# A two-layer graph network: the leaky step and the float16 split of z moved from the middle stage into layer 1

## The reference, cut to what matters

```
x = layernorm(x + L0(x, adj))                       # x: 8 x 2048 x 64
# layer 1: 8 batches x 4 heads = 32 instances of attention over 2048 nodes
h    = einsum('bnc,hdc->bhnd', x, Wh)
s    = where(mask, h h^T, -1e16)
cat  = softmax(s) h + bh                            # per instance 2048 x 64
z    = leaky_relu(cat, 0.2)                         # = max(cat, 0.2 cat)
# middle stage
h2   = einsum('bnk,dk->bnd', z, Wo)                 # 256 -> 64 columns
# layer 2: 8 instances of the same attention, one per batch
out2 = softmax(where(mask, h2 h2^T, -1e16)) h2 + bo
out  = layernorm(leaky_relu(out2, 0.2)) * gamma + beta
x    = layernorm(x + out)
```

## Time and profile before

| | us |
|---|---|
| three runs, median (lowest to highest) | 3323.97 (3322.51 to 3327.71) |
| the profiled execution, its time | 3323.41 |
| its span, first to last instruction | 3321.7 |
| PE busy | 3065.0 (92% of the span) |
| DVE busy | 2739.8 (82%) |
| ACT busy | 2369.3 (71%) |
| POOL busy | 2546.0 (77%) |
| granted clock of PE, mean | 0.976 of full speed |

### The profile page before, as it was taken

One profiled execution on the slowest core, in us unless ns is written; L12 is line 12 of the kernel. 1 busy time (PEld: TensorE's weight loads), 2 busy tenths in 40 slices (PEclk: granted clock), 3 DMA queues, 4 the chain that ended last, 5 costly groups with the idle time before them and its releaser, 6 DMA issues. The chain is left out here.

```text
span 3321.7 us, 126248 instructions
## 1 busy us (share of the span) xinstructions
PE 3065.0 (92%) x49399; PEld 2287.0 (69%) x49399; DVE 2739.8 (82%) x5344; ACT 2369.3 (71%) x2806; POOL 2546.0 (77%) x1861
## 2 busy tenths in 40 slices
PE   5856799999999999999999999999986699999997
PEld 3425577777777777777777777777765577777775
DVE  6664688888888888888888888888877599898998
ACT  1146677777777777777777777777766588787886
POOL 1136598989999999899999999999976257676775
PEclk8979999999999999999999999999998899999998
DMA  5207889998899889999988998899867433332321
GB/s 207 67 1 271 223 156 153 165 161 163 155 164 169 157 156 173 159 159 161 167 164 155 163 166 165 154 166 166 163 122 235 165 124 134 119 130 115 132 116 73
DMA packets 1189166, 507.67 MB, mean 153 GB/s; under 512 B 1090718, under 2 KB 1148508, under 8 KB 1186588
## 3 DMA queue, kind: packets, MB, share of 16 engines
q1 hardware_dynamic: 1187564, 497.60, 70.8%
q0 software_dynamic: 1200, 3.93, 0.3%
HBM read 102.12 MB, written 62.91 MB: 50 GB/s over the span
## 5 line engine op out<-in xcount | busy, mean ns | idle before, releaser
L633 POOL TENSOR_TENSOR mask_slot<-probs 128x1024 f16<-128x1024 f32 x1024 | 1916.1, 1893 | 221.8 <-ACT probs L1017 138.4
L1017 ACT ACTIVATE probs<-scores,shifted_max 128x2048 f32<-128x2048 f32 x512 | 1026.1, 2004 | 166.6 <-DVE shifted_max L1222 159.0
L1217 DVE CUSTOM_DVE_ANT_0 scores<-ps,mask 128x1024 f32<-128x1024 f32 x512 | 625.5, 1222 | 202.4 <-PE ps L860 196.5
L859 PE MATMUL ps<-operands 128*128 128x512 f16 x2048 | 777.3, 380 | 1.7 <-DVE neg_max L1217 1.7
L860 PE MATMUL ps<-operands 128*128 128x512 f16 x2048 | 776.7, 379 | 0.0
L1022 ACT COPY probsT<-ps 128x1024 bf16<-128x1024 bf16 x512 | 518.0, 1012 | 359.3 <-PE ps L868 359.3
L1217 DVE CUSTOM_DVE_ANT_0 scores<-ps,mask,neg_max 128x1024 f32<-128x1024 f32 x512 | 657.3, 1284 | 103.4 <-issue 57.7
L868 PEld LDWEIGHTS ps<-ident,probs 128*128 128x128 bf16 x8192 | 519.6, 98 | 294.7 <-issue 160.7
L868 PE MATMUL ps<-ident,probs 128*128 128x128 bf16 x8192 | 624.2, 219 | 8.3 <-issue 3.7
L879 PE MATMUL ps<-v_parts,probsT 128*128 128x64 f16 x8192 | 547.6, 193 | 0.0
L878 PE MATMUL ps<-v_parts,probsT 128*128 128x64 f16 x8192 | 547.2, 193 | 0.0
(11 more groups left out here) (175 smaller groups left out, 4575.1 us busy)
## 6 DMA issues: line engine op xcount, KB each, us to landing
mask_slot<-mask SPq DMA_DIRECT2D x129, 512.0 KB, 2.9
operands<-hT_d SPq DMA_DIRECT2D x40, 512.0 KB, 4.1
operands<-hT_d SPq DMA_DIRECT2D x80, 256.0 KB, 4.6
v_parts<-h_d SPq DMA_DIRECT2D x40, 512.0 KB, 4.6
scores<-in_adj SPq DMA_DIRECT2D x16, 1024.0 KB, 4.8
h_d<-probs SPq DMA_DIRECT2D x32, 512.0 KB, 3.5
hT_d<-probs SPq DMA_DIRECT2D x32, 512.0 KB, 2.8
probsT<-mask_slot SPq DMA_TRANSPOSE x1024, 3.6
```

The lines of the kernel that those rows point to most:

```text
L633: pool.tensor_tensor(low[:, u, w], probs[:, u, w], high[:, u, w], ALU.subtract).then_inc(sem(f"low{half}"), 1)
L859: pe.matmul(ps[:, b, :], hi_lo[:, p, t * P:(t + 1) * P], hi_lo[:, p, w], start=True, stop=False)
L1017: act.activation(probs[:, 1 - u, :], scores[:, 1 - u, :], ACT.Exp, bias=shifted_max[:, 1 - u:2 - u], scale=-1.0, accum_out=row_sum[:, held ...
L1217: dve.tensor_tensor_reduce(scores[:, u, w], ps[:, 2 * c:2 * c + 2, :].rearrange("p a n -> p (a n)"), mask[:, t * N + c * 2 * BANK:t * N + ...
```

## The change

z is finished where layer 1 empties PSUM. DVE's four bias additions go to `scratch` instead of `outs`. One step later ACT writes 0.2 times that to the same PSUM bank (`out_fifth`) and DVE takes the maximum there (`out_leaky`); another step later ACT copies it as float16 into the high half in `outs` (`out_high`); another step later DVE subtracts for the low half and `out_copied` is given, three steps later than before. FLUSH goes from 5 to 8 steps. The store of an instance has the same 512 KB, now two float16 halves per value.

In the middle stage the leaky step, the high half and the low half go away, and with them POOL's part. The loads go to the buffers `z_parts` that PE flips from, and the load for unit k+4 waits for PE's flip of unit k (`p2_zT`) instead of POOL's subtraction (`p2_zlo`). The first four loads go out together after the last exponential.

```
-FLUSH = 5
+FLUSH = 8
...
-        z_d = dram("z_d", [P, LAYER1, NT * D], F32)
+        z_d = dram("z_d", [P, LAYER1, NT * P], F16)
...
+        def z_halves(held, k, part):
+            return outs[:, held, :].bitcast(F16).rearrange("p (t k d) -> p t k d", k=2, d=D)[:, 4 * k:4 * k + 4, part, :]
+        def group_at(back, lag):
+            if back(lag) and back(lag)[2] % 4 == 3:
+                old, held, tt = back(lag)
+                return old, held, tt // 4, old * 4 + tt // 4 + 1
+            return None
+        def group_bank(k):
+            return ps[:, 6 + k % 2, 0:4 * D]
+        def group_tmp(k):
+            return scratch[:, k % 2 * 4 * D:(k % 2 + 1) * 4 * D]
...
             def load_z(b, w):
-                sp.dma_start(z_in(w).rearrange("p (h n) -> p h n", h=H),
+                sp.dma_start(z_parts(w).rearrange("p (h n) -> p h n", h=H),
...
             def p2_step(k, w, b):
                 if within(k + 4):
-                    sp.wait_ge(sem("p2_zlo"), k + 1)
+                    sp.wait_ge(sem("p2_zT"), k + 1)
                     gate(sp, "sp")
                     load_z(b + 1, w)
...
-            load_z(0, 0)
+            sp.wait_ge(sem("exp_done"), LAYER1 * NT)
+            for w in range(4):
+                load_z(0, w)
             store_z(LAYER1 - 1, 1)
             for u in range(2):
                 for half in range(2):
                     sp.wait_ge(sem(f"low_turned{half}{u}"), turns(LAYER1 * NT - 2 + u, u))
-            load_z(0, 1)
-            load_z(0, 2)
             for u in range(2):
                 sp.wait_ge(sem(f"z_stored{u}"), 8 * LAYER1)
-            load_z(0, 3)
...
-            def p2_step(k, w, b):
-                pool.wait_ge(sem("p2_zhi"), k + 1)
-                gate(pool, "pool")
-                pool.tensor_tensor(z_split(w, 1), z_columns(w), z_split(w, 0), ALU.subtract).then_inc(sem("p2_zlo"), 1)
-            quads(pool, p2_step)
...
             def turn_z(k, w):
                 u = w % 2
-                pe.wait_ge(sem("p2_zlo"), k + 1)
+                pe.wait_ge(sem(f"z_in{w}"), (k - w) * 4 + 16)
...
+                if group_at(back, 5):                   
+                    old, held, k, n = group_at(back, 5)
+                    act.wait_ge(sem("out_biased"), n)
+                    act.activation(group_bank(k), group_tmp(k), ACT.Copy, scale=0.2).then_inc(sem("out_fifth"), 1)
+                if group_at(back, 6):
+                    old, held, k, n = group_at(back, 6)
+                    act.wait_ge(sem("out_leaky"), n)
+                    if k == 0:
+                        since(act, sem(f"z_stored{held}"), (old - held) * 8)
+                    act.copy(z_halves(held, k, 0), by_tile(group_bank(k))).then_inc(sem("out_high"), 1)
...
-                if within(k + 3):
-                    head_z(k + 3, (w + 3) % 4)
...
-            for w in range(3):
-                head_z(w, w)
...
-                        added = dve.scalar_tensor_tensor(outs[:, held, tt * D:(tt + 1) * D], out_slot(tt), row_inv[:, held, tt:tt + 1],
+                        added = dve.scalar_tensor_tensor(group_tmp(k)[:, tt % 4 * D:(tt % 4 + 1) * D], out_slot(tt), row_inv[:, held, tt:tt + 1],
...
-                    added.then_inc(sem("out_copied"), 1)
+                    added.then_inc(sem("out_biased"), 1)
+                if group_at(back, 5):
+                    old, held, k, n = group_at(back, 5)
+                    dve.wait_ge(sem("out_fifth"), n)
+                    dve.tensor_tensor(group_bank(k), group_bank(k), group_tmp(k), ALU.max).then_inc(sem("out_leaky"), 1)
+                if group_at(back, 7):
+                    old, held, k, n = group_at(back, 7)
+                    dve.wait_ge(sem("out_high"), n)
+                    dve.tensor_tensor(z_halves(held, k, 1), by_tile(group_bank(k)), z_halves(held, k, 0), ALU.subtract).then_inc(sem("out_copied"), 1)
...
-                if within(k + 4):
-                    leaky_z(k + 4, w)
...
-            for w in range(4):
-                leaky_z(w, w)
```

More of the change, by code:

```diff
@@ L192, in stage16, with by_tile @@
             return buffer[:, u, at // 2:(at + n) // 2].bitcast(F16)
+        def by_tile(ap):
+            return ap.rearrange("p (t c) -> p t c", c=D)
         def x_parts(u):
@@ L198, in xT_parts @@
             return stage16(scores, u, G * P, G * P)
-        def z_in(w):
-            return (outs[:, 0, :], mask_slot[:, 0, :].bitcast(F32), mask_slot[:, 1, :].bitcast(F32), outs[:, 1, :])[w]
         def z_parts(w):
             return stage16(scores, w // 2, w % 2 * H * G * P, H * G * P)
[L207 to L211, removed]
+        def z_halves(held, k, part):
[9 more added lines that the diff above has]
+            return scratch[:, k % 2 * 4 * D:(k % 2 + 1) * 4 * D]
         def zT_parts(u):
@@ L473, in store_z @@
                 gate(sp, "sp")
-                sp.dma_start(z_d[:, i, :] if isinstance(i, int) else z_d[:, bass.ds(i, 1), :], outs[:, p, :]).then_inc(sem(f"z_stored{p}"), 16)
+                sp.dma_start(z_d[:, i, :] if isinstance(i, int) else z_d[:, bass.ds(i, 1), :], outs[:, p, :].bitcast(F16)).then_inc(sem(f"z_stored{p}"), 16)
             def layer1_step(g, i, t, p, back):
@@ L498, in load_z @@
             def load_z(b, w):
-                sp.dma_start(z_in(w).rearrange("p (h n) -> p h n", h=H),
-                             z_d[:, b * H:(b + 1) * H, w * G * D:(w + 1) * G * D] if isinstance(b, int) else
-                             z_d[:, bass.ts(b, H), w * G * D:(w + 1) * G * D]).then_inc(sem(f"z_in{w}"), 16)
+                sp.dma_start(z_parts(w).rearrange("p (h n) -> p h n", h=H),
+                             z_d[:, b * H:(b + 1) * H, w * G * P:(w + 1) * G * P] if isinstance(b, int) else
+                             z_d[:, bass.ts(b, H), w * G * P:(w + 1) * G * P]).then_inc(sem(f"z_in{w}"), 16)
             def store_h2(b, w):
@@ L1235, in layer1_step @@
                     dve.wait_ge(sem("inverse"), old * 4 + k + 1)
-                    if k == 0:
-                        gate(dve, "dve")
-                        since(dve, sem(f"z_stored{held}"), (old - held) * 8)
                     gate(dve, "dve")
                     for tt in range(4 * k, 4 * k + 4):
-                        added = dve.scalar_tensor_tensor(outs[:, held, tt * D:(tt + 1) * D], out_slot(tt), row_inv[:, held, tt:tt + 1],
+                        added = dve.scalar_tensor_tensor(group_tmp(k)[:, tt % 4 * D:(tt % 4 + 1) * D], out_slot(tt), row_inv[:, held, tt:tt + 1],
                                                          bias[:, old, :] if isinstance(old, int) else bias[:, bass.ds(old, 1), :].rearrange("p o d -> p (o d)"),
                                                          ALU.mult, ALU.add)
-                    added.then_inc(sem("out_copied"), 1)
+                    added.then_inc(sem("out_biased"), 1)
[7 more added lines that the diff above has]
+                    dve.tensor_tensor(z_halves(held, k, 1), by_tile(group_bank(k)), z_halves(held, k, 0), ALU.subtract).then_inc(sem("out_copied"), 1)
             dve.wait_ge(sem("mask_ready"), NT)
```

3 lines of the change are left out of this document (removed).

## The result

| | before | changed |
|---|---|---|
| median, us (range, runs) | 3323.24 (3322.42 to 3327.71, 4) | 3359.11 (3351.38 to 3364.7, 4) |
| ratio, 95% interval | | 1.0104 (1.0081 to 1.0126) |
| profiled execution, us; its span | 3323.41; 3321.7 | 3364.7; 3362.9 |
| first product of the middle stage to its product 28, us | 88.83 | 132.58 |

Slower, as forecast, but by 35.9 us where the forecast had 15.5, and above the range. The spans differ by 41.2 us, and the timeline of PE divides that: layer 1 ends 3.4 later (its last group of matmuls starts at 2499.06 instead of 2495.69), from there to the first product takes 8.2 less (5.41 instead of 13.61), from the first product to product 28 takes 43.75 more, and what follows 2.3 more. So all but the 3.4 us, to which run 11 comes back, lies in the middle stage and just behind product 28.

What follows compares the result with a forecast made beforehand. PE was taken to bound layer 1 and a chain of waits the middle stage. 3323.4 + 0 (layer 1) + 15.5 (middle stage's start and pace) = 3338.9 us; range 3324 to 3353.

Steps and rivals of the forecast that it cites:

- Layer 1, cost 0: Layer 1: DVE's added maximum and subtraction fit its idle gaps, the maximum by 0.10 us; ACT's work covered; cost 0.
- Rival 3: Layer 1: each maximum takes 0.2 us more than priced, 13 us on top of the forecast, total 3352; chance 0.18.
- Start of the middle stage, gain 8.65: Middle stage's start: PE flips once z has landed; first product at 2500.65 instead of 2509.30, gain 8.65 us.
- The first two units: Middle stage's start: first intervals kept at 4.56 and 3.1 us, products of k=1 at 2505.2, k=2 at 2508.3.
- The chain of the pace: Middle stage: SP's load waits for PE's flip, h2's store follows, ACT's cast, then PE wait: 4.05 us per unit, not 3.12.
- Rival 2: Middle stage: SP's new wait does not reach ACT; only the 8.65 us gain remains, total 3314.8; chance 0.09.
- Landing of h2: Middle stage: h2's store lands behind the 512 KB load, 4.3 us after the load's issue, at E+4.5; cast 0.1 later.
- The bound E+3.5: Middle stage: h2's store lands 2.0 us after its own issue at E+1.5, as if nothing stood ahead.
- rival 1: Middle stage: stores land as if alone, 7.1 us per two units, total 3325.9; chance 0.20.
- 13 x 8.1: Middle stage: 8.1 us per two units from k=2 to product 28, 105.3 us, product 28 at 2613.6.
- The sum: Whole kernel: 3323.4 + 0 for layer 1 + 15.5 for start and pace together = 3338.9 us.
- Rival 4: Middle stage: clock drops to 1.2 GHz, 1.6 us more per two units, 21 us more, total 3360; chance 0.07.

Runs made afterwards that it cites:

- run 11: The changed kernel itself, unchanged, measured once more: 3356.3 us, 1.0100 of the kernel before.
- Run 8: Changed kernel with four h2 buffers and without layer 1's scaling, maximum, high cast and subtraction: 3313.5 us, 0.9983 of the kernel before.
- run 9: run 4 with each group's maximum in layer 1 done twice, the second behind a wait for the first: 3331.4 us, 1.0026 of the kernel before.
- run 10: run 4 with each group's subtraction in layer 1 done twice, the second behind a wait: 3325.7 us, 1.0007 of the kernel before.
- run 1: Changed kernel with SP's two stores issued ahead of the wait and the load: 3317.3 us, 0.9989 of the kernel before.
- run 2: Changed kernel with SP's wait first, then both stores, the load last: 3317.6 us, 0.9984 of the kernel before.
- run 3: Changed kernel whose load, still ahead of the stores, is for unit k+3, its buffer flipped a unit ago: 3315.3 us, 0.9989 of the kernel before.
- run 4: Changed kernel with four h2 buffers instead of two, SP's order kept: 3309.5 us, 0.9970 of the kernel before.
- run 5: Changed kernel with 12 extra, overwritten matmuls per middle-stage unit while PE waits: 3333.9 us, 1.0041 of the kernel before.
- run 6: run 1 with PE flipping z two units ahead and those copies ahead of h2's cast and subtraction: 3296.2 us, 0.9929 of the kernel before.
- run 7: run 6 with four h2 buffers: 3287.1 us, 0.9897 of the kernel before.

## Why the prediction was right and wrong

- **Layer 1, cost 0: right.** The forecast took 0.43 us for a maximum that fits by 0.10; it takes 0.42 and fits by 0.11 (0.45 to the masking, 0.34 where it is held back). Run 8 shows the cost, none; runs 9 and 10 show that the margin was real and thin. Rival 3 did not happen; its size, 13 us for 0.2 us more per maximum, has the order of run 9's 19 us for 0.46.
- **Start of the middle stage, gain 8.65: right.** 8.2 in the profiled execution, counted from the end of layer 1.
- **The first two units: too short by 1.75 us.** They take 9.40 us, where the forecast kept the 7.65 of the kernel before. In both kernels the clock is at its low level after the end of layer 1 (granted 0.5 from 2495.4 to 2512.5 us before, from 2499.2 to 2512.8 in the changed kernel). The changed kernel's first product comes 4.8 us earlier, so both units fall into that time, where I had let only one be. Runs 1 to 4, without the long waits, have the same 9.40, and in runs 8 and 9, where the low clock ended sooner (after 6.8 and 10.2 us instead of 13.65), they take 7.45 and 7.80: it belongs to the start and not to the pace.
- **The chain of the pace: right.** SP's gated load ahead of h2's store, ACT's cast behind that store, PE behind ACT. Runs 1 to 4 each cut one link, and the stage is back at 91 to 94 us. Rival 2 said that the wait does not reach ACT. It missed by far: without the wait the cast comes 2.3 us after the flip's end (mean of the kernel before and of run 4), with it 5.07.
- **Landing of h2: too early by 0.3 us.** The forecast has the cast at E+4.6, E being the end of the flip. In run 5, where the clock is full, it comes at E+4.88 (mean of k=2 to 27; in the rows shown E is 2579.62 and the cast at 2584.56, E+4.94), and then 1.57 to the product instead of 1.5. Per two units 8.49 us on the mean of k=2 to 28, instead of 8.1: 13 x 0.39 = 5 us. The bound E+3.5, rival 1, falls, and with it what I had said for it: the 2.0 us of the kernel before were also those of a store behind a load, only issued later after it. The Trainium skill, "DMA: Bandwidth & Descriptors", section on queues, rings and completion order, says that a completion's increment lands only after every earlier write of its DMA engine. The traces agree: between 2510 and 2600 no h2 store landed ahead of the load before it in the kernel before, the changed one and runs 1 to 8, and with loads that take much the same (3.6 to 3.9 us) the store lands the sooner, the later it goes out after one: in 3.3 us when it goes out 1.25 after the load (changed kernel), 2.7 at 1.9 (run 1), 1.8 at 2.75 (run 2), medians of that stretch. What the prediction names "the second case below" in that place is its rival 1.
- **The clock: the step that failed.** The forecast's term "13 x 8.1" took product and flip at 0.94 and 1.06 us, that is at full clock. I had seen what a low clock would add, 1.6 us per two units, and put it in a rival of its own with 0.07, as if it were an alternative to the forecast. It is a consequence: the waits that the forecast itself predicts leave PE idle for 3.2 us at a time, and the granted clock fell with that; in runs 1 to 4, where PE waits 1.7 us at most for a copy, it stayed full from product 2 to product 28. From k=2 to 28 two units take 9.48 us, against 8.49 with PE kept busy: 13 x 0.99 = 13 us. Only about half of it is PE's own time: from a product to the end of the next flip pass 2.57 us on the mean instead of 2.05. The rest lies in the cast, 5.07 after the flip instead of 4.88, and in the way from it to the product, 1.81 instead of 1.57. In the pair shown a flip at the low clock ends late, the next is on time, the two loads go out 3.1 us apart, and the second store takes 4.2 us to land instead of 3.3.
- **The sum.** 113.0 us were forecast for the stage (2500.65 to 2613.6), 132.6 measured: 5 for the landing, 13 for the clock, 1.75 at its start make the 19.6 missing. The medians differ by 35.9 us, 20.4 more than the forecast's 15.5. Rival 4, the forecast with the low clock on top, said 3360, and 3359.1 were measured. That is in part luck: it had 21 us for the clock alone, which took 13, and nothing for the landing and the first two units.

The share of the clock rests on run 5. Its extra matmuls could add time of their own, but PE still waits for the copy behind them, 0.60 and 0.69 us in the rows shown and 0.1 or more in every unit from 7 to 28, so in the steady part they add none. How much idle time brings the clock down, and why it falls in about every second unit and not in all, was not tried.

## What to carry to other kernels

On SP's queue, which is worked off in order, a load that waited for an engine delayed the stores behind it twice: until its wait ended, and again by its own bytes. Look for who needs such stores, and put them first or give their source more buffers (two more here). When a forecast says that PE will sit idle in a loop for microseconds, give the low clock a price as part of that forecast, not as a rival to it. And where a wait in a loop is shorter than a unit, ask first whether the producer can run one unit ahead: here that was worth 20 to 24 us (run 6 against 1, run 7 against 4), while the change with its waits mended gained 11 at best (run 4).

## What the runs showed of the hardware

- Work of no use made a kernel faster: 12 matmuls per unit in PE's idle time raised the granted clock from 0.84 to 0.98 between 2510 and 2590, and cut the time from 1.0104 to 1.0041 of the kernel before.
- Two delays that lengthen the stage by 2.7 us (run 2) and 0.7 us (run 3) alone, against run 1, lengthen it by 41.7 together. Alone each leaves the store in time, or nearly, within a unit of 3.1 us; together they don't, and then the clock adds to it.
- A 128 KB store on SP's queue landed 0.7 to 0.85 us (medians) after the 512 KB load issued ahead of it, in every kernel looked at and whether it was issued 1.25 or 2.75 us after that load.
- DVE's maximum with a PSUM result took 423 ns for 128x256 (mean of 128), the subtraction of the same size out of PSUM to SBUF 414. ACT's scaling of that size into PSUM took 367, its casts out of PSUM 351 (layer 1) and 372 (middle stage). So no price of a PSUM result shows, though the pairs differ in operation and type too.
